# Gram blocks dealt out over rolling PSUM banks, row writes on ScalarE's queue, zeroing paced by row tiles, and the first aggregation sources rounded ahead of the last product

## The reference, cut to what matters

```
xn  = layernorm(x)
s   = segment_sum((xn @ W)[src] * edge_weight, dst)       # aggregation
q,k = xn @ Wq.T + bq, xn @ Wk.T + bk ; each divided by its norm over ALL elements
phi(t) = exp(einsum(weights, t)) * exp(-sum(t*t)/2) / sqrt(64)
m   = rowsum_per_head(phi(q)*phi(k)) ; mix = m * v / m     # v = xn @ Wv.T + bv
x   = x + s + mix
x   = x + bitlinear_ffn(layernorm(x))                      # int8-like activations, ternary weights
```

## Time and profile before

| what | value |
|---|---|
| median of 3 runs | 1821.58 us |
| the profiled execution: its time, its span | 1823.07 us, 1821.3 us |
| PE busy | 1705.3 us (94%) |
| DVE, ACT, POOL busy | 1097.2, 513.7, 580.5 us |
| mean granted TensorE clock | 0.975 of full speed |

### The profile page before, as it was taken

The page is one execution under the profiler, slowest core; times in us unless marked ns, Lnnn a source line. Parts: engine busy times, 40 slices in busy tenths (PEclk is TensorE's granted clock), DMA queues, the critical chain, the costliest instruction groups (busy, mean ns, idle before and its releaser), DMA issues.

```text
span 1821.3 us, 23768 instructions
## 1 busy us (share of the span) xinstructions
PE 1705.3 (94%) x8178; PEld 1372.3 (75%) x8178; DVE 1097.2 (60%) x2537; ACT 513.7 (28%) x610; POOL 580.5 (32%) x392
## 2 busy tenths in 40 slices
PE   5199998899999999999999997999999999999797
PEld 5188987787777787877777775878878787776465
DVE  5176545346677776663566654458475674855764
ACT  3153221032211111112322222233333333333443
POOL 2013556835577777777665000000000000000000
PEclk9599999999999999999999998999999999999899
DMA  9898786324445566654887657224545244453455
GB/s 334 352 376 307 248 290 162 50 46 118 121 113 118 121 181 144 142 133 92 232 236 200 196 182 212 94 91 135 137 134 145 92 144 124 142 136 92 129 164 158
DMA packets 150388, 301.58 MB, mean 166 GB/s; under 512 B 60220, under 2 KB 86892, under 8 KB 150332
## 3 DMA queue, kind: packets, MB, share of 16 engines
q1 hardware_dynamic: 83576, 231.56, 39.7%
q0 software_dynamic: 61824, 52.62, 14.2%
q10 hardware_dynamic: 4932, 16.73, 3.5%
HBM read 203.80 MB, written 97.05 MB: 165 GB/s over the span
## 4 chain that ended last, share of the span: by engine, by line
PE 88%; DMA 3%; DVE 3%; SPq 3%; issue 1%; ACT 1%; DVEq 0%; ACTq 0%
PE PS L356 22%; PE PS L355 22%; PE PS L354 22%; PE PS L1280 5%; PE PS L1278 5%; PE PS L1281 5%; PE PS L1491 4%; PE PS L1516 2%; PE PS L1349 2%; DMA xnT<-XT 2%; DMA Aside<-A_dense 1%; SPq L98 1%; SPq L437 1%; PE PS L1294 1%; ACT hqT L884 1%
## 5 line engine op out<-in xcount | busy, mean ns | idle before, releaser
L662 POOL DMA_INDIRECT A_dense<-wtot,cell x336 | 537.0, 1598 | 278.3 <-DMA A_dense<-wtot,cell 129.6
L354 PE MATMUL PS<-SL,AH 125*125 125x512 f32 x800 | 316.2, 395 | 12.8 <-DVE AL L1125 12.8
L355 PE MATMUL PS<-SH,AL 125*125 125x512 f32 x800 | 317.4, 397 | 0.0
L356 PE MATMUL PS<-SH,AH 125*125 125x512 f32 x800 | 316.9, 396 | 0.0
L354 PE MATMUL PS<-WL,xtH 128*125 128x512 f32 x640 | 252.6, 395 | 2.7 <-DVE WL L1062 2.7
L356 PE MATMUL PS<-WH,xtH 128*125 128x512 f32 x640 | 252.4, 394 | 0.0
L355 PE MATMUL PS<-WH,xtL 128*125 128x512 f32 x640 | 252.2, 394 | 0.0
L1122 DVE TENSOR_TENSOR SL<-S,SH 125x1024 fp32r<-125x1024 f32 x100 | 122.4, 1224 | 167.1 <-ACT SH L823 166.9
L823 ACT ACTIVATE SH<-S 125x1024 fp32r (+1 forms) x100 | 106.0, 1060 | 312.6 <-PE PS L356 312.6
L354 PEld LDWEIGHTS PS<-SL,AH 125*125 125x125 f32 x800 | 149.2, 186 | 53.4 <-DVE AL L1125 15.1
L355 PEld LDWEIGHTS PS<-SH,AL 125*125 125x125 f32 x800 | 149.6, 187 | 37.4
(11 more groups left out here) (172 smaller groups left out, 2577.5 us busy)
## 6 DMA issues: line engine op xcount, KB each, us to landing
A_dense<-zeros POOLq DMA_DIRECT2D x40, 1280.0 KB, 9.5
xt<-xnT SPq DMA_DIRECT2D x62, 500.0 KB, 6.2
Araw<-A_dense SPq DMA_DIRECT2D x100, 250.0 KB, 2.7
Aside<-A_dense SPq DMA_DIRECT2D x100, 250.0 KB, 2.9
keyrow<-key_rows SPq DMA_DIRECT2D x42, 512.0 KB, 3.7
ewrow<-weight_rows SPq DMA_DIRECT2D x42, 512.0 KB, 5.6
xnT<-XT SPq DMA_DIRECT2D x20, 500.0 KB, 8.5
zx<-in_x SPq DMA_DIRECT2D x22, 448.0 KB
```

The source lines that it names most:

```text
L354: nc.tensor.matmul(o, lh, rl, start=start, stop=False)
L355: nc.tensor.matmul(o, ll, rh, start=False, stop=False)
L356: return nc.tensor.matmul(o, lh, rh, start=False, stop=stop)
L662: pool.indirect_dma_start(cells[m], bass.IndirectOffsetOnAxis(cell[:, col:col + 1], 0), wtot[:, col:col + 1], None, compute_op=ALU.add).th ...
```

## The change

1. **Gram blocks.** The block of rows 0 and columns 512 to 640 moves from `G_LEFT` to `G_RIGHT`, where its mirror image is computed with row block 4 against columns 0 to 128 and 512 to 640 (one strided operand, 256 wide). Both two-column segments go: the sums' columns are now part of wider segments. Left: four segments, 512, 386, 512, 386. Right: nine segments in seven banks.
2. **Rolling banks.** Banks are numbered through all passes (position modulo 8). PE waits for a bank when it opens it (`bank_ready`), its reader when the bank closes (`bank_done`, new semaphore `s_bank`), not for the pass.
3. **Row writes** go out on ScalarE's queue, write n - 1 behind the copy of tile n. SyncE loads the first key rows as soon as the keys are written, and the six Wq rows after Gram item 14.
4. **Zeros.** Strip r of A_dense0 waits for Gram item min(3r, 20).
5. **Norm.** `bdqk` in four halves, the fold starts on the first two; a dummy square root on ScalarE ahead of the real one.
6. **Aggregation.** The sources of the first pair go into buffers of their own, laid over `xt`, `xtH0` and other dead space. They are rounded once tile 18 is multiplied, both splits ahead of stage 4's last tile on VectorE; the dummy reloads are gone; A pairs are loaded earlier against z and `wT`. `iedge` and `wst` change place.

```
-G_LEFT = [(0, 0, 512, 0, 0), (0, 512, 1024, 1, 0), (1, 128, 640, 2, 0), (1, 640, EXT, 3, 0), (0, D, EXT, 3, 386)]
+G_LEFT = [(0, 0, 512, 0, 0), (0, 640, EXT, 1, 0), (1, 128, 640, 2, 0), (1, 640, EXT, 3, 0)]
+G_RIGHT = [(2, 256, 768, 0, 0), (2, 768, EXT, 1, 0), (7, 896, EXT, 1, 258), (3, 384, 896, 2, 0), (3, 896, EXT, 3, 0),
+           (6, 768, EXT, 3, 130), (4, None, 256, 4, 0), (4, 640, EXT, 5, 0), (5, 640, EXT, 6, 0)]
...
+    def bank_ready(eng, pos):
+        if pos >= 8 + NB:
+            eng.wait_ge(s_bs, pos - 8 - NB + 1)
+        elif pos >= 8:
+            eng.wait_ge(s_gev, GEV[pos - 8])
+    def bank_done(eng, n, b):
+        if b == (NR if n % 2 else NL) - 1:
+            eng.wait_ge(s_gm, (TILES, G_ITEMS, G_ITEMS + KT, G_ITEMS + 2 * KT, G_ITEMS + 3 * KT, ITEMS)[n])
+        else:
+            eng.wait_ge(s_bank, n // 2 * (NB - 2) + (NL - 1 if n % 2 else 0) + b + 1)
...
-        sp.wait_ge(s_st, 6)
+        sp.wait_ge(s_kout, 32)
+        for b in range(2):
+            load_key_rows(sp, b, b)
+        sp.wait_ge(s_gm, 14)
         for n in range(6):
             load_raw(n, s_raw[0])
-        for t in range(TILES):
-            sp.wait_ge(s_xev[t % 2], t // 2 + 1)
-            sp.dma_start(xnT_d[t]...)
...
         for r in range(STRIPS):
-            if r >= 4:
-                pool.wait_ge(s_gm, r - 3)
+            if r:
+                pool.wait_ge(s_gm, min(3 * r, TILES))
...
+        def write_transposed(n):
+            act.wait_ge(s_xev[n % 2], n // 2 + 1)
+            act.dma_start(xnT_d[n]..., XT[:, n % GT]...).then_inc(s_xTout[n % GT], 16)
...
             transposed_rows(n)
+            if n:
+                write_transposed(n - 1)
...
+                if first and opens:
+                    bank_ready(pe, base + bank)
...
+                if last_one and closes and s + 1 < len(segments):
+                    last.then_inc(s_bank, 1)
...
-        for i in range(2):
-            act.wait_ge(s_mm[i], 3 * HALF)
-        with act.Fori(0, HALF) as h:
+        act.wait_ge(s_mm[0], 3 * HALF)
+        act.wait_ge(s_xtl[1], 3 * HALF)
+        high_of_pair(0, 0)
+        act.wait_ge(s_mm[1], 3 * HALF)
+        with act.Fori(1, HALF) as h:
...
         low_of_sources(0, 0, 0)
+        low_of_sources(1, 1, 0)
         stage4_tile(9, 1)
-        low_of_sources(1, 1, 0)
...
         wait_stage4(sp)
+        load_next_A(1)
         split_rows(sp, zr[:, :, :], z_d[0:GN, :]..., s_zin)
         for f in range(3):
-            if f:
-                load_next_A(f)
+            load_next_A(f + 2)
             sp.dma_start(wT[:, f], ...)
```

More of the change, by code:

```diff
@@ L549, in stage4_tile @@
             sp.wait_ge(s_xtl[i], h + 2 * HALF + 1)
-            load_tile(nxt, i)
+            if not isinstance(h, int) or t + 2 < TILES:
+                load_tile(nxt, i)
+            elif i:
+                load_next_A(0)
             if chunk is None and isinstance(h, int) and t < 6:
@@ L727, in _ @@
                                      ACT.Copy).then_inc(s_ev0, 1)
+        write_transposed(TILES - 1)
         high_of_rows(TILES + 1)
-        act.wait_ge(s_gm, TILES)
         act.wait_ge(s_kout, 32)
-        evacuate_gram(LEFT_BANKS, LEFT_SCALES, 0, range(4))
+        for b in range(NL):
+            evacuate_gram(0, b)
         for n in range(TILES + 2, G_ITEMS):
@@ L750, in _ @@
             high_of_weights(0, j)
[L751 to L756, removed]
+        for b in range(NR):
+            evacuate_gram(1, b)
+            if b in (2, 4):
+                high_of_weights(0, 1 + b // 2)
         nc.scalar.activation(raw[:, KT:2 * KT, D:EXT], bias[:, 1], ACT.Copy).then_inc(s_ev0, 1)
@@ L978, in low_of_weights, with weigh @@
                                     ALU.subtract).then_inc(s_lo, 1)
[L980 to L983, removed]
+        def weigh(m, right):
+            for b, n in enumerate(RIGHT_WIDTHS if right else LEFT_WIDTHS):
+                bank_done(dve, 2 + 2 * m + right, b)
+                at = b + right * NL
+                o = PS[:, ((1 + m) * NB + at) % 8, 0:n]
+                nc.vector.scalar_tensor_tensor(o, o, 1.0, Gs[:, at, 0:n], ALU.mult, ALU.mult,
+                                               accum_out=parts[:, m, at:at + 1]).then_inc(s_bs, 1)
         for j in range(KT):
@@ L1012, in _ @@
         dve.wait_ge(s_norm, 4)
[L1013 to L1016, removed]
+        for half in (slice(0, KT // 2), slice(KT // 2, KT)):
+            for m in range(2):
+                nc.vector.tensor_scalar(bdqk[:, m, half].rearrange("p k n -> p (k n)"),
+                                        bd[:, half].rearrange("p k n -> p (k n)"),
+                                        norms[:, 2, m:m + 1], None, ALU.mult).then_inc(s_bdq, 1)
+        nc.vector.tensor_tensor(norms[:, 3, :], PS[:, 1, 0:2], norms[:, 2, :], ALU.mult).then_inc(s_norm, 1)
         dve.wait_ge(s_norm, 5)
@@ L1270, in transposes, with gram @@
             return last
[L1272 to L1276, removed]
-                cols = slice(i * P, (i + 1) * P)
[L1278 to L1281, removed]
+        def gram(n, hi, lo, first, last_one):
+            right = n % 2
+            segments, base = (G_RIGHT, NL) if right else (G_LEFT, 0)
+            base += n // 2 * NB
+            for s, (i, a, b, bank, at) in enumerate(segments):
+                opens = s == 0 or segments[s - 1][3] != bank
+                closes = s + 1 == len(segments) or segments[s + 1][3] != bank
+                if first and opens:
+                    bank_ready(pe, base + bank)
+                cols = slice(i * P, (i + 1) * P)
+                if a is None:
+                    o = PS[:, (base + bank) % 8, at:at + 2 * P].rearrange("p (a n) -> p a n", a=2)
+                    rh, rl = (v[:, 0:D].rearrange("p (a n) -> p a n", a=2)[:, :, 0:P] for v in (hi, lo))
+                else:
+                    o = PS[:, (base + bank) % 8, at:at + b - a]
+                    rh, rl = hi[:, a:b], lo[:, a:b]
+                nc.tensor.matmul(o, hi[:, cols], rl, start=first and opens, stop=False, skip_group_check=True)
+                nc.tensor.matmul(o, lo[:, cols], rh, start=False, stop=False, skip_group_check=True)
+                last = nc.tensor.matmul(o, hi[:, cols], rh, start=False, stop=last_one, skip_group_check=True)
+                if last_one and closes and s + 1 < len(segments):
+                    last.then_inc(s_bank, 1)
             last.then_inc(s_gm, 1)
@@ L1445, in sources @@
             pe.wait_ge(s_lo5[i], m + 1)
+            sh, sl = SH[0:ROWS, i, :], SL[0:ROWS, i, :]
+            if isinstance(m, int) and m == 0:
+                sh, sl = (b[0:ROWS, :] for b in first_S[i])
             for d in ORDER:
@@ L1458, in sources, with aggregate @@
             last.then_inc(s_pe5[i], 1)
-        with pe.Fori(0, GROUPS) as g:
+        def aggregate(g):
             for i in range(2):
@@ L1467, in _ @@
                 sources(g, i, g * HALF + HALF - 1, False, i == 1)
+        aggregate(0)
+        with pe.Fori(1, GROUPS) as g:
+            aggregate(g)
         pe.wait_ge(s_wT, 64)
```

143 lines of the change are left out of this document (64 added, 79 removed).

## The result

The changed kernel takes 1742.6 us (median of 4 runs, 1741.89 to 1743.44) against 1821.6 for the kernel before (median of 3 runs). The ratio is 0.9566, with a 95% interval of 0.9538 to 0.9595; a fourth, disturbed run of the kernel before (3440 us) is left out. Forecast were 1736 and a range of 1727 to 1757; the measured time lies 6.6 us above the forecast and just outside the narrower 1729 to 1742, to which I gave 58%. The profiled execution took 1743.0 us, its span is 1741.2.

The account below looks back on a forecast made before the run. PE, busy 94% of the span, was taken to bound the kernel. Savings of 45.0 + 6.8 + 8.0 + 10.7 + 14.9 = 85.4 us from 1823.1 gave 1737.7, forecast as a 1736 median; range 1727 to 1757, narrower 1729 to 1742 (58%).

Parts of the forecast that it names:

- The term 45.0: Left row pass: 45.0 us saved from PE's 36.6 us wait, lost clock and shorter tiles; ends 40 and 47.
- nothing of 3 MB stands ahead of them any more: Left row pass: argument against row writes staying at 28.2 us, a slower-than-before rival (1832 us) given 2%.
- the landing of 3.9 us by a third of the rate: Left row pass: ScalarE's queue gets about a third of 392 GB/s, so a 0.51 MB write takes 3.9 us.
- the 1.4 us of catching up for VectorE: Left row pass: VectorE is behind after the keys' transposes, so PE waits about 1.4 us once, subtracted from the gain.
- bytes bound the row pass: Rival, left row pass: 35.6 MB must move until its end; up to 11 us of gain lost, about 1745; 15%.
- the same jam forms on ScalarE's queue in part: Rival, left row pass: the change does little, half of the 40 us stays, 1757 us; 4%.
- writes land late: Rival, left row pass: PE waits for writes taking 13 us, 4.3 per tile, 13 us lost, 1750; 8%.
- Segments and seams: Other Gram passes, their seams and the norm: 6.8 us from right items, 8.0 from left items, 10.7 from seams.
- The wait at Wk: Seam at the first Wk item: of 5.24 us waiting for `weigh`, 1.2 saved and 4.0 stay, in its second segment.
- Zeros: Later zeros end between 155 and 215 us, scatters start then, cost 0; rival that POOL bounds the aggregation 1%.
- Aggregation and fold: Aggregation's start: 3.28, 8.91 and 3.7 us of clock saved, 1.0 new waiting, net 14.9; fold 0.7 from `bdqk` halves.
- the wait moves to `wT`: Rival, aggregation: its long wait moves to `wT`; 9 us lost, 1745 us; 12%.

Follow-up runs that it names:

- the keys moved: The changed kernel with the two small-packet key and edge-weight writes issued on SyncE's queue instead of ScalarE's: 1734.28 us, ratio to the kernel before 0.9502.

## Why the prediction was right or wrong

**Left row pass: the one wrong term.** The term 45.0 was mis-sized: 38.4 was measured. The step that failed is "nothing of 3 MB stands ahead of them any more", with the landing of 3.9 us by a third of the rate. I counted what had stood ahead of the row writes on SyncE's queue and saw it leave; I didn't list what already stood on the queue that they moved to. The key writes were even in front of me: the 635 packets of 0.31 MB in the earlier trace rows are the same ones. Read as small packets in the turns, they gave me the share of the rate; read as work ahead of write 3, they would have given the stop. With the keys moved, 48.9 us are gained (the last matmul at 139.41 and 90.52), above my upper end of 47. So the late write cost about 9.5 us (the 10.5 between the two left ends less the 1 of the earlier start), and the term missed by only 6.6 because its other parts were too low by some 3: in that respect the size of the miss is luck. With the keys moved the excess over 45.0 is 3.9, in three parts: the tile (3.44 in pairs with VectorE against 3.5, and 3.32 instead of 3.41 for PE alone, together about 1.3), 1.9 us of earlier X rows, and the 1.4 us of catching up for VectorE, of which only 0.5 appears (waits for `ring` 3.9, of which 3.4 are in the kernel before too).

**Rival "bytes bound the row pass".** Its mechanism bounds the tiles only with the old pacing of the zeros (3.7 us a tile), and there it costs about 5 us; in the changed kernel POOL's bytes lengthen the one stop by 2.8. What happened instead is nearest to "the same jam forms on ScalarE's queue in part", to which I gave 4% and 20 us; it took about 9.5.

**Rival "writes land late".** Most writes do take 9 us instead of 3.9, and PE doesn't wait, since three tiles last 10.3. A write doesn't have its queue to itself: ScalarE's queue moves 5.18 MB from 66 to 100 us in the changed kernel, 152 GB/s, at which 0.51 MB take 3.4 us, as long as a tile. So the 9 us are mostly time behind the one or two row writes ahead (an estimate from this rate). At 10.5 us a write held ScalarE for 1.7 us once, and at 11 us a write the tiles went 3.7 us apart (zeros paced as before): the rival was near, and the pacing of the zeros keeps it off.

**Segments and seams: right.** 25.5 forecast and measured. The wait at Wk kept 3.96 (forecast 4.0), the norm 0.9 (0.95); the halves of `bdqk` gave 0.4 instead of 0.7 (2.1 became 1.7). Undoing parts puts 3.3 us at the norm on the signal per bank, and the waits for `Gs` and two of `weigh` on the rolling numbers.

**Zeros: right.** The first scatter is at 171 us (forecast 155 to 215), the last at 940.7 instead of 988.9, and PE's waits for `AL`, 0.5 us in all, leave no room for a late matrix.

**Aggregation and fold: right in kind, 1.3 short.** Up to the aggregation's start 3.5 us were gained (forecast 3.28), inside it 11.1 (forecast 8.91 + 3.7 - 1.0 = 11.6). The rest, 1.9, lies in the fold (37.4 us before, 35.5 after), and my sum had named it without counting it: clock lost behind the norm's stop. The first stretch of the fold before (the columns are those of the earlier trace rows):

```profile
365.50:370.00 4.50, 4.50 (x23) 4.50 (x24) 0.17 (x2) 0.00 (x0) 3.08 (x3) 0.56 0.49 117
```

and after:

```profile
301.60:306.00 4.40, 4.37 (x39) 4.37 (x40) 0.99 (x4) 0.49 (x1) 2.67 (x2) 1.00 1.02 316
```

The granted clock was 0.56, near 1.2 GHz, behind stops of 3.9 and 2.1 us, and stays at 2.4 GHz behind the stops of 0.9 and 1.7: 4.5 x 0.44 = 2.0 us. But this trace of the changed kernel was lucky. In five of the experiments PE makes the same stops (0.9, then 1.4 to 1.6 us), and the clock still falls. The same stretch of the fold with the keys moved, its stops 0.9 and 1.5:

```profile
289.70:294.20 4.50, 4.44 (x27) 4.45 (x28) 1.38 (x5) 0.00 (x0) 0.51 (x1) 0.67 1.04 383
```

There the fold takes 37.1 us, 0.3 less than before; in five other experiments it takes 35.5, as in the changed kernel. So the change is worth 0.3 to 1.9 us here, and which of the two a run gets wasn't found. The rival "the wait moves to `wT`" didn't come.

**What stays open.** Why the first X rows arrive 0.9 to 1.9 us earlier than before was not tried; over all traces of the changed kernel and its edits the first tile starts at 22.4 to 24.1 us (24.3 in the one trace before), so part of it is scatter. The 8.91 us are rebuilt to 7.3; the last 1.6 were not.

## What to carry to other kernels

When a transfer moves to another queue, list what stands ahead of it there, in packets as well as in bytes: 0.34 MB in half-kilobyte pieces cost more than 3.1 MB of long ones on a queue of their own. Hold the slowest transfer whose slot is wanted again, not the median, against what a ring of slots gives it: here four slots gave three tiles, 10.3 us; writes of 9 us were free and writes of 11 us set the pace. Price each stop of a few microseconds with the half-speed stretch behind it, at every seam and not only at the large ones, and look at more than one trace before you count that stretch as gained.

## What was unexpected of the hardware

Small writes hold up the long one behind them far beyond their bytes: 0.34 MB ahead made a 0.51 MB write take 21.2 us, and it took at most 13.9 without them, at nearly the same total rate (375 and 395 GB/s). And a stop of 3.9 us cost about half as much again: 3.9 + 2.0 at the Wk seam. Ahead of the fold, stops of 0.9 and 1.4 to 1.7 us in a row left the clock at 2.4 GHz in six traces and halved it for a while in five, which cost 1.6 us.
